# Gate logits from fp16 halves, and VectorE's five weight halves cut in two pieces each

## The chip, the cores and the metric
The kernel runs on one core of a Trainium2 chip, in one launch. The metric is the device time of that launch in microseconds. Inside the core TensorE (PE), VectorE (DVE), ScalarE (ACT) and GpSimd (POOL) run their own instruction streams, SyncE (SP) and some of the others start DMA transfers, and everything is tied together by semaphores that are written by hand.

## The reference, cut to what matters
```
x = x + attention(layernorm(x), ctx)            # 8 x 256 tokens, 512 wide, 32 heads, 8 key/value groups
h = layernorm(x)
logits = h @ gate_weight.T                      # 512 -> 8 experts, float32
scores = softmax(logits)                        # group limited: 2 of 4 groups, then top 2 of 8 experts
e_n = (silu(h @ gate_w[n].T) * (h @ up_w[n].T)) @ down_w[n].T          # n = 0..7, 352 wide
shared = (silu(h @ sh_gate_w.T) * (h @ sh_up_w.T)) @ sh_down_w.T       # 704 wide
x = x + sum_n weight_n * e_n + shared
```
The float32 products are made from fp16 halves: a value is scaled by a power of two and split as high = fp16(v), low = fp16(v - high), and three of the four half products are summed. In the kernel before, the gate logits are one of the products still made in float32 directly.

## The kernel before, in words
The 2048 tokens are 16 tiles of 128. The work runs in stages: projections and attention to about 283 us, the token stage from there to about 377 us, then the feed-forward stage (two shared experts, then 36 slots of routed rows, then the shared experts for the other half of the tokens).

**The token stage**, around which the change sits, takes the tiles in order; the numbers t below are tiles. All orders are written out by hand.
- PE, per tile t: `ln_transpose(t-2)` (L1457), `ot_transpose(t+1)` (L1440), `out_project(t)` (8 float32 instructions, L1448), `gate(t-3)` (8 float32 instructions of 8 columns with 128x128 weights, L1466). The gate waits for ACT's float32 copy of the transposed tile, `lnt_evac`. The last three gates stand between the first matmuls of the feed-forward stage.
- ACT, per tile: `lnt_out(t-2)` writes the high half of the transposed normalised tile (L1084) and a float32 copy of it, lnT (L1085); `ot_evac(t+1)` (L1079), which `out_project(t+1)` waits for; `std2(t)` (L1093), `gate_out(t-3)` (L1089), `first_part(t-2)` for t = 2 to 11, the high half of the weight half h = t-2 (L1119, after its load has landed); then `ln2_out(t)` (L1098), the normalised tile, which waits for DVE.
- DVE, per tile: `residual_norm(t)`, from the residual add (L1985) to the shift (L1994), with the low half of tile t-2 in its middle (`cut_rows`, L1971). In odd tiles 3 to 11 it then makes the low half of the weight half h = t-2 in one instruction of 1408 columns (`second_part`, L2019).
- POOL makes the low halves of the even h = 0 to 8 in two instructions of 1408 columns (scale, L838; subtract, L848), in order of h. After each h, even or odd, it starts the load of h+3 (L829, 704 KB) into the stage buffer that h has freed; for odd h it first waits for DVE's count `gu_cut_v`.
- SP, per tile: load of the attention rows of t+5, store of the two halves of tile t-2, store of the residual rows, load of the residual rows for t+2 (L563), store of the normalised rows.

The weights have been scaled by powers of two that are found in the attention stage and at the start of the token stage (`down_scales`, 10 columns, one for each expert).

## Time and profile before
| | us |
|---|---|
| median of 3 runs (753.55 to 754.98) | 754.7 |
| the profiled execution: its own time | 754.92 |
| the profiled execution: its span | 753.1 |
| PE busy | 732.2 (97%) |
| DVE busy | 561.1 (75%) |
| ACT busy | 419.0 (56%) |
| POOL busy | 272.1 (36%) |
| matmuls of the gate, L1466, x128 | 15.3 busy |

The span is what the profiler recorded from the first to the last instruction; the time is some 1.8 us longer. Busy time of an engine is an average over stages with different limits, so the stage tables and the timelines further down say more than this table. The granted clock of TensorE is 0.998 of full speed over the run.

### The profile page before, as it was taken

To read this page: it belongs to the slowest core of one execution; us is meant where nothing else is said; L and a number is where in the kernel's file an instruction comes from. 1 tells how busy PE (TensorE), PEld (TensorE's weight loads), DVE (VectorE), ACT (ScalarE), POOL (GpSimd) and SP (SyncE) were. 2 spreads that over 40 slices of the span, in tenths; PEclk is the share of its full clock that TensorE was granted. 3 is DMA by queue.
4 is the path that set the end of the run, shared out by engine and by line. 5 is a ranking of instruction groups with operands and counts; after the bars stand their busy time and mean duration, and the time that the engine had idled before them with its cause. 6 is when DMAs were issued, how large, how long until landed. Compare 5 with 4: busy or idle time off the path is not lost.

```text
span 753.1 us, 16125 instructions
## 1 busy us (share of the span) xinstructions
PE 732.2 (97%) x5325; PEld 398.9 (53%) x5326; DVE 561.1 (75%) x1191; ACT 419.0 (56%) x845; POOL 272.1 (36%) x221
## 2 busy tenths in 40 slices
PE   6998999999999999999999999999999999999998
PEld 3554533434444334656665566555555556655554
DVE  4777689999999967788589998655555555546776
ACT  3667468888888884777543454343433334223222
POOL 3264006999997311664400401212111121016540
PEclk9999999999999999999999999999999999999999
DMA  9898946755755798997578664977767779549993
GB/s 328 332 409 282 252 147 187 221 168 176 220 150 151 249 344 301 345 386 281 190 204 259 153 155 123 197 175 181 184 168 184 173 180 213 127 124 283 329 308 92
DMA packets 155100, 168.17 MB, mean 223 GB/s; under 512 B 97952, under 2 KB 111776, under 8 KB 154528
## 3 DMA queue, kind: packets, MB, share of 16 engines
q1 hardware_dynamic: 143724, 126.20, 57.6%
q0 software_dynamic: 10720, 40.12, 17.0%
q10 hardware_dynamic: 596, 1.07, 0.4%
q8 instruction: 36, 0.59, 0.4%
q14 instruction: 24, 0.20, 0.1%
HBM read 104.09 MB, written 41.42 MB: 193 GB/s over the span
## 4 chain that ended last, share of the span: by engine, by line
PE 53%; DVE 23%; DMA 8%; issue 6%; POOL 4%; ACT 3%; SPq 2%; DVEq 0%; POOLq 0%; ACTq 0%
PE psum L1521 21%; DVE sb_rows L1786 12%; PE psum L1538 11%; PE psum L1523 4%; PE psum L1448 4%; PE psum L1257 4%; POOL sb_weights L952 4%; DMA sb_weights<-k_parts 2%; DMA sb_weights<-in_wdn 2%; PE psum L1540 2%; PE psum L1233 1%; DVE sb_rows L1915 1%; PE psum L1281 1%; DMA x_dram<-sb_rows 1%; DMA sb_rows<-xb_dram 1%
## 5 line engine op out<-in xcount | busy, mean ns | idle before, releaser
L1521 PE MATMUL psum<-sb_weights,sb_rows 128*128 128x352 f16 (+1 forms) x1344 | 209.7, 313 | 0.0
L1521 PEld LDWEIGHTS psum<-sb_weights,sb_rows 128*128 128x128 f16 x1344 | 131.2, 98 | 76.1 <-issue 1.2
L1786 DVE TENSOR_REDUCE sb_rows<-psum 128x4 f32<-128x1024 f32 x128 | 150.0, 1214 | 4.6 <-PE psum L1281 4.5
L1073 ACT ACTIVATE sb_weights<-psum 128x512 f32<-128x512 f32 x256 | 139.4, 595 | 22.8 <-PE psum L1353 19.7
L1538 PE MATMUL psum<-sb_weights,sb_hT 128*128 128x512 f16 (+1 forms) x522 | 122.2, 379 | 0.0
L1147 ACT ACTIVATE psum<-psum 128x352 f32<-128x352 f32 x68 | 30.5, 448 | 124.9 <-DVE psum L2040 112.3
L933 POOL DMA_INDIRECT sb_rows<-xn_rows,sb_slot_tok x36 | 34.6, 960 | 176.7 <-DVE sb_rows L2418 134.8
L1353 PE MATMUL psum<-sb_weights 50*128 50x512 f16 x256 | 86.6, 387 | 1.7 <-ACT sb_weights L1073 0.9
L1367 PE MATMUL psum<-sb_weights 128*32 128x256 f32 x1024 | 82.6, 394 | 0.3
L1538 PEld LDWEIGHTS psum<-sb_weights,sb_hT 128*128 128x128 f16 x522 | 50.9, 98 | 54.0 <-issue 0.6
L1281 PE MATMUL psum<-sb_weights 48*128 48x256 f16 x512 | 70.7, 274 | 1.6 <-DMA sb_weights<-k_parts 0.9
L1448 PE MATMUL psum<-sb_weights 128*128 128x512 f32 x128 | 58.3, 598 | 0.5 <-ACT sb_weights L1079 0.4
L2053 DVE SCALAR_TENSOR_TENSOR sb_h<-psum,sb_h_scale_i,sb_h 128x352 f16<-128x352 f32 x68 | 39.7, 583 | 22.7 <-ACT sb_h L1152 19.5
L952 POOL DMA_INDIRECT sb_weights<-slot_y,sb_p_i x32 | 32.5, 1015 | 64.4 <-DMA slot_y<-sb_rows 41.9
L2040 DVE SCALAR_TENSOR_TENSOR psum<-psum,sb_inv_now,sb_h 128x352 f32<-128x352 f32 x36 | 21.3, 592 | 43.6 <-issue 31.0
L1353 PEld LDWEIGHTS psum<-sb_weights 50*128 50x128 f16 x256 | 23.4, 93 | 54.2 <-ACT sb_weights L1073 44.7
L1142 ACT ACTIVATE sb_h<-psum,sb_inv_now 128x352 f32<-128x352 f32 x36 | 20.0, 555 | 49.4 <-PE psum L1521 37.7
L1257 PE MATMUL psum<-sb_weights 128*128 128x512 f16 x192 | 44.9, 380 | 2.3 <-DVE sb_weights L1852 1.2
L1152 ACT ACTIVATE sb_h<-psum,sb_h_scale_i 128x352 f16<-128x352 f32 x68 | 37.7, 555 | 16.2 <-DVE sb_h_scale_i L2045 14.8
L838 POOL TENSOR_TENSOR sb_weights<-sb_weights,sb_w_scale_i 128x1408 f32<-128x1408 f32 x15 | 38.0, 2533 | 23.6 <-ACT sb_weights L1119 22.8
L848 POOL TENSOR_TENSOR sb_weights<-sb_weights 128x1408 f16<-128x1408 f32 x15 | 43.0, 2864 | 1.2
L1142 ACT ACTIVATE sb_h<-psum,sb_w_inv_i 128x352 f32<-128x352 f32 x32 | 17.8, 556 | 33.1 <-PE psum L1521 22.7
(307 smaller groups left out, 1172.8 us busy)
## 6 DMA issues: line engine op xcount, KB each, us to landing
sb_weights<-in_wgu SPq DMA_DIRECT2D x20, 704.0 KB, 7.1
sb_weights<-in_wgu POOLq DMA_DIRECT2D x20, 704.0 KB, 6.8
sb_weights<-in_wdn SPq DMA_DIRECT2D x17, 768.0 KB, 6.3
slot_y<-sb_rows SPq DMA_DIRECT2D x36, 256.0 KB, 2.4
sb_weights<-q_parts SPq DMA_DIRECT2D x96, 64.0 KB, 3.0
x_dram<-sb_rows SPq DMA_DIRECT2D x24, 256.0 KB, 4.6
q_parts<-sb_weights SPq DMA_DIRECT2D x16, 256.0 KB, 4.1
sb_rows<-in_x POOLq DMA_DIRECT2D x16, 256.0 KB, 5.8
```

Source lines behind the costliest of these rows:

```text
L848: nc.gpsimd.tensor_tensor(low, stage, high, ALU.subtract).then_inc(gu_cut, 1)
L952: nc.gpsimd.indirect_dma_start(out=to, out_offset=None, in_=slot_y, in_offset=bass.IndirectOffsetOnAxis(ap=idx[:, t:t + 1], axis=0)).then_ ...
L1073: nc.scalar.activation(probs[G % 2][:, kt, pair * 512:(pair + 1) * 512], bank[4 + f % 2], ACT.Exp, scale=exp_by[n]).then_inc(exp_done, 1)
L1257: mm = nc.tensor.matmul(bank[Q_BANKS[n][m]], wq16[:, wp, k, m * P:(m + 1) * P], xnT[n % 2][:, xp, k, :], start=(k == 0 and i == 0), stop=( ...
L1281: mm = nc.tensor.matmul(bank[banks[qt] + side][:, h * SEQ:(h + 1) * SEQ], q_st[s][lo:hi, g, h, b * SEQ + qt * P:b * SEQ + (qt + 1) * P], k ...
L1353: nc.tensor.matmul(bank[4 + side].rearrange("p (h t) -> p h t", h=HH), k_st[s][lo:hi, g, b * SEQ + kt * P:b * SEQ + (kt + 1) * P], q_st[s] ...
L1367: mm = nc.tensor.matmul(bank[6][VW * c:VW * (c + 1), 0:SEQ], v_now, probs[G % 2][:, kt, c * SEQ:(c + 1) * SEQ], start=(kt == 0), stop=(kt ...
L1448: mm = nc.tensor.matmul(bank[2 + s][:], oT[s][:, k, :], wfc_sb[:, k, :], start=(k == 0), stop=(k == KD - 1))
L1521: mm = nc.tensor.matmul(to[:, 0:F], x_T[:, at:at + P], gu(wp, k, which), start=first, stop=last)
L1538: mm = nc.tensor.matmul(bank[Y_BANKS[par]][:], hT[par][:, hp, j, :], dn(wp, j), start=first, stop=last)
L1786: nc.vector.tensor_reduce(to[:, :, j // UB, :, j % UB, qt], psum[:, banks[qt] * 512:(banks[qt] + 2) * 512] .rearrange("p (a h k) -> p a h ...
L2053: nc.vector.scalar_tensor_tensor(h16[par][:, 1, 0:F], bank[GU_BANKS[par][1]][:, 0:F], h_scale[:, par:par + 1], h16[par][:, 0, 0:F], ALU.mu ...
```

## The change
Gate: lnT and ACT's copy of it are gone. `gate(t)` multiplies both fp16 halves of the tile (high and low, which exist for the experts anyway) with one operand of 16 columns, the high and the low half of the gate weights: again 8 instructions, now fp16. The two groups of 8 sums go to two planes of `route` and are added on DVE ahead of the softmax. The gate now waits for DVE's low half (`ln16_done`) in place of ACT's copy. The scale of the gate weights is an eleventh column of the table of the down weights; its maximum is taken in the attention stage, and three small DVE instructions make the halves after tile 2 (`gate_halves`).

Pieces: the low half of an odd h was made in tile h+2; now its first 704 columns are made in tile h+2 and its last 704 in tile h+3. `gu_cut_v` counts pieces, so those who waited for h now wait for the second piece.

```
-        lnT = [row(6), row(7)]
-        xb_sb = lnT
+        xb_sb = [row(6), row(7)]
+        gw16 = wsel[...][:, 0:KD * NE].bitcast(F16).rearrange("p (k s e) -> p k s e", k=KD, s=2)
...
                 if w == 2:                                    # SP, feed-forward stage
-                    sp.wait_ge(gu_cut_v, HELD)
+                    sp.wait_ge(gu_cut_v, 2 * HELD)
...
                 else:                                         # POOL, odd h
-                    pool.wait_ge(gu_cut_v, h // 2 + 1)
+                    pool.wait_ge(gu_cut_v, h + 1)
...
-                nc.scalar.activation(ln16[s][:, 0:D], bank[4 + s][:], ACT.Copy, scale=X_SCALE)
-                nc.scalar.copy(lnT[s], bank[4 + s][:]).then_inc(lnt_evac, 1)
+                nc.scalar.activation(ln16[s][:, 0:D], bank[4 + s][:], ACT.Copy, scale=X_SCALE).then_inc(lnt_evac, 1)
...
-                nc.scalar.copy(logits[:, bass.ds(t, 1), :], bank[6 + s][:, 0:NE].unsqueeze(1)).then_inc(gate_evac, 1)
+                nc.scalar.activation(route[:, 0:2, bass.ds(t, 1), :], bank[6 + s][:, 0:2 * NE]..., ACT.Copy,
+                                     scale=dn_inv[:, NE + SH:DN_TOPS]).then_inc(gate_evac, 1)
...
             def gate(t, s):
-                pe.wait_ge(lnt_evac, t + 1)
+                pe.wait_ge(ln16_done, t + 1)
...
                 for k in range(KD):
-                    mm = nc.tensor.matmul(bank[6 + s][:, 0:NE], lnT[s][:, k * P:(k + 1) * P], gw_sb[:, k, :], ...)
+                    for part in range(2):
+                        at = part * D + k * P
+                        mm = nc.tensor.matmul(bank[6 + s][:, 0:2 * NE], ln16[s][:, at:at + P], gw16[:, k]..., ...)
...
                 if t == 3:
+                    pe.wait_ge(scale_done, 5)
                     gate(0, 0)
...
+                if G == 3:                                    # DVE, attention stage
+                    dve.wait_ge(w_fc, 48)
+                    nc.vector.tensor_reduce(dn_max[:, NE + SH:DN_TOPS], gw_sb[:]..., AX.X, ALU.max, apply_absolute_value=True)
...
+            def gate_halves():
+                g = slice(NE + SH, DN_TOPS)
+                dve.wait_ge(scale_done, 2)
+                nc.vector.tensor_scalar(dn_inv_i[:, g], dn_inv_i[:, g], float(10 << 23), None, ALU.subtract).then_inc(scale_done, 1)
+                nc.vector.tensor_scalar(gw16[:, :, 0, :], gw_sb[:], dn_scale[:, g], None, ALU.mult).then_inc(scale_done, 1)
+                dve.wait_ge(scale_done, 4)
+                nc.vector.scalar_tensor_tensor(gw16[:, :, 1, :], gw_sb[:], dn_scale[:, g], gw16[:, :, 0, :],
+                                               ALU.mult, ALU.subtract).then_inc(scale_done, 1)
...
-            def second_part(h):
+            def second_piece(h, n):
                 dve.wait_ge(gu_first, CUTS_P2 + h + 1)
                 high, low = cut_place(h)
+                here = slice(n * HALF // 2, (n + 1) * HALF // 2)
+                nc.vector.scalar_tensor_tensor(low[:, here], stage_p3[h % 3][:, here], w_scale[:, h // 2:h // 2 + 1],
+                                               high[:, here], ALU.mult, ALU.subtract).then_inc(gu_cut_v, 1)
             for t in range(2, TILES):
                 residual_norm(t, t % 2, t // 2)
-                if t % 2 == 1 and t < 2 * HELD + 2:
-                    second_part(t - 2)
+                if t == 2:
+                    gate_halves()
+                if 3 <= t < 2 * HELD + 3:
+                    h = t - 2 - (t + 1) % 2
+                    second_piece(h, (t + 1) % 2)
...
             def softmax_in():
                 dve.wait_ge(gate_evac, TILES)
+                link(nc.vector.tensor_tensor(logits, logits, score, ALU.add))
```

## Rows read from the trace of the kernel before
**Rows 1.** Stage table: stretch, busy time (instructions) per engine, clock, DMA share, GB/s.
```profile
298.00:350.00 52.00, 51.53 (x234) 31.53 (x232) 42.38 (x104) 39.01 (x69) 30.89 (x17) 1.00 1.01 368
325.00:346.00 21.00, 21.00 (x97) 13.12 (x97) 18.21 (x46) 15.70 (x29) 12.52 (x8) 1.00 1.04 385
```
**Rows 2.** Chain of waits, one tile of the token stage: start, length, what.
```profile
330.20 3.49 PE psum L1448 x8
333.69 0.79 PE psum L1466 x8
334.48 0.49 PE psum L1457 x4
334.97 0.44 PE psum L1440 x4
```
**Rows 3.** TensorE's timeline, weight loads of 32 narrow fp16 matmuls in the feed-forward stage.
```profile
426.85 0.47 PEld L1608 LDWEIGHTS psum<-sb_ln_sb,sb_rows 128*128 128x128 f16 x16
```
**Rows 4.** DVE's timeline, tiles 9 to 12.
```profile
329.38 0.68 DVE L1985 TENSOR_TENSOR sb_rows<-psum,sb_rows 128x512 f32<-128x512 f32 x1
333.73 0.69 DVE L1985 TENSOR_TENSOR sb_rows<-psum,sb_rows 128x512 f32<-128x512 f32 x1 [0.87 <-ACT sb_rows L1098]
337.25 2.64 DVE L2019 SCALAR_TENSOR_TENSOR sb_weights<-sb_weights,sb_w_scale_i 128x1408 f16<-128x1408 f32 x1
339.81 0.68 DVE L1985 TENSOR_TENSOR sb_rows<-psum,sb_rows 128x512 f32<-128x512 f32 x1
```
**Rows 5.** POOL's timeline, the even half h = 6.
```profile
332.94 2.53 POOL L838 TENSOR_TENSOR sb_weights<-sb_weights,sb_w_scale_i 128x1408 f32<-128x1408 f32 x1 [2.64 <-ACT sb_weights L1119]
335.55 2.86 POOL L848 TENSOR_TENSOR sb_weights<-sb_weights 128x1408 f16<-128x1408 f32 x1
338.70 0.58 POOL L829 DMA_DIRECT2D sb_weights<-in_wgu  x1 [0.30 <-POOL sb_weights L848]
```
**Rows 6.** The same op of DVE as in rows 4, in tiles 5 and 11, and POOL beside it.
```profile
316.68 1.69 DVE L2019 SCALAR_TENSOR_TENSOR sb_weights<-sb_weights,sb_w_scale_i 128x1408 f16<-128x1408 f32 x1 [1.11 <-ACT sb_weights L1119]
313.84 2.86 POOL L848 TENSOR_TENSOR sb_weights<-sb_weights 128x1408 f16<-128x1408 f32 x1
347.62 2.76 DVE L2019 SCALAR_TENSOR_TENSOR sb_weights<-sb_weights,sb_w_scale_i 128x1408 f16<-128x1408 f32 x1
346.04 2.86 POOL L848 TENSOR_TENSOR sb_weights<-sb_weights 128x1408 f16<-128x1408 f32 x1
```
**Rows 7.** The same kind of DVE op at 512 columns (count: min/median/max ns).
```profile
L2285 DVE SCALAR_TENSOR_TENSOR sb_weights<-sb_zero_row,sb_dn_scale_i,sb_weights x1: 741/741/741, 462.1 to 462.1; 128x512 f16<-128x512 f32 x1
```
**Rows 8.** DMA of L829: all ten (count, size, median us to landing), then those after 299 us.
```profile
sb_weights<-in_wgu POOLq DMA_DIRECT2D x10, 704.0 KB, 7.7
...
DMA to landing us min/median/max: 6.8/7.6/9.3
```
**Rows 9.** Timelines: ACT in tile 5, DVE in tile 6, and the projection of tile 8.
```profile
315.18 1.47 ACT L1119 ACTIVATE sb_weights<-sb_weights,sb_w_scale_i 128x1408 f16<-128x1408 f32 x1 [0.98 <-DMA sb_weights<-in_wgu]
318.95 0.69 DVE L1985 TENSOR_TENSOR sb_rows<-psum,sb_rows 128x512 f32<-128x512 f32 x1 [0.58 <-DMA sb_rows<-xb_dram]
324.79 3.70 PE L1448 MATMUL psum<-sb_weights 128*128 128x512 f32 x8
```
**Rows 10.** Chain of waits, from the last tile to the feed-forward stage.
```profile
364.58 0.70 DVE sb_rows L1985
369.47 0.48 ACT sb_rows L1085
371.92 3.75 PE psum L1521 x24
```
**Rows 11.** TensorE's timeline: the gate issued after the projection of tile 12.
```profile
349.17 0.95 PE L1466 MATMUL psum<-sb_gw_sb,sb_rows 128*128 128x8 f32 x8
```
**Rows 12.** Small terms: POOL's wait for the gate weights, and a 128x128 op of DVE.
```profile
116.50 0.55 POOL L872 DMA_DIRECT2D sb_rows<-in_x  x1 [0.47 <-DMA sb_gw_sb<-in_gwT]
377.74 0.29 DVE L2076 TENSOR_TENSOR sb_route<-sb_route,sb_t_tile 128x128 f32<-128x128 f32 x1
```

More of the change, by code:

```diff
@@ L81 @@
 CUT_W = 8
+DN_TOPS = NE + SH + 1
 PA, PB, PC = SH * EARLY, SLOTS, SH * (TILES - EARLY)
@@ L223, in build @@
         a_in += [dn_tail[:], bfc_sb]
-        dn_max = sb("dn_max", [P, NE + SH])
-        dn_max_all = sb("dn_max_all", [NE + SH, 1])
-        dn_exp = sb("dn_exp", [P, NE + SH], I32)
-        dn_scale_i = sb("dn_scale_i", [P, NE + SH], I32)
-        dn_inv_i = sb("dn_inv_i", [P, NE + SH], I32)
+        dn_max = sb("dn_max", [P, DN_TOPS])
+        dn_max_all = sb("dn_max_all", [DN_TOPS, 1])
+        dn_exp = sb("dn_exp", [P, DN_TOPS], I32)
+        dn_scale_i = sb("dn_scale_i", [P, DN_TOPS], I32)
+        dn_inv_i = sb("dn_inv_i", [P, DN_TOPS], I32)
         dn_scale, dn_inv = dn_scale_i[:].bitcast(F32), dn_inv_i[:].bitcast(F32)
@@ L276, in build @@
         res_in, x2_sb, xn2_sb = [row(0), row(1)], [row(2), row(3)], [row(4), row(5)]
-        lnT = [row(6), row(7)]
-        xb_sb = lnT
+        xb_sb = [row(6), row(7)]
         ln16 = [zero_row[:].bitcast(F16), ln16_sb[:].bitcast(F16)]
-        w_max_rows = row(6)[0:NE + SH, 0:P]
+        w_max_rows = row(6)[0:DN_TOPS, 0:P]
         tok_in, xT, mid, late = [row(0), row(1)], [row(2), row(3)], [row(4), row(5)], [row(6), row(7)]
@@ L305, in build @@
         wsel = sb("wsel", [P, TILES, NE])
+        gw16 = wsel[:].rearrange("p t e -> p (t e)")[:, 0:KD * NE].bitcast(F16).rearrange("p (k s e) -> p k s e", k=KD, s=2)
         sel = sb("sel", [P, TILES, NE])
@@ L1083, in lnt_out @@
                 act.wait_ge(lnt_stored[s], stored * 16 + FREE)
-                nc.scalar.activation(ln16[s][:, 0:D], bank[4 + s][:], ACT.Copy, scale=X_SCALE)
-                nc.scalar.copy(lnT[s], bank[4 + s][:]).then_inc(lnt_evac, 1)
+                nc.scalar.activation(ln16[s][:, 0:D], bank[4 + s][:], ACT.Copy, scale=X_SCALE).then_inc(lnt_evac, 1)
             def gate_out(t, s):
                 act.wait_ge(gate_ready, t + 1)
-                nc.scalar.copy(logits[:, bass.ds(t, 1), :], bank[6 + s][:, 0:NE].unsqueeze(1)).then_inc(gate_evac, 1)
+                nc.scalar.activation(route[:, 0:2, bass.ds(t, 1), :],
+                                     bank[6 + s][:, 0:2 * NE].rearrange("p (s e) -> p s e", s=2).unsqueeze(2), ACT.Copy,
+                                     scale=dn_inv[:, NE + SH:DN_TOPS]).then_inc(gate_evac, 1)
             def std2(t):
@@ L1465, in gate @@
                 for k in range(KD):
-                    mm = nc.tensor.matmul(bank[6 + s][:, 0:NE], lnT[s][:, k * P:(k + 1) * P], gw_sb[:, k, :],
-                                          start=(k == 0), stop=(k == KD - 1))
+                    for part in range(2):
+                        at = part * D + k * P
+                        mm = nc.tensor.matmul(bank[6 + s][:, 0:2 * NE], ln16[s][:, at:at + P],
+                                              gw16[:, k].rearrange("p s e -> p (s e)"),
+                                              start=(k == 0 and part == 0), stop=(k == KD - 1 and part == 1))
                 mm.then_inc(gate_ready, 1)
@@ L1481, in _ @@
                     pe.wait_ge(dn_max_done, NE + SH)
-                    nc.tensor.transpose(bank[5][0:NE + SH, 0:P], dn_max[:], ident[:]).then_inc(w_max_t, 1)
+                    nc.tensor.transpose(bank[5][0:DN_TOPS, 0:P], dn_max[:], ident[:]).then_inc(w_max_t, 1)
                 else:
                     pe.wait_ge(w_max_b, 2)
-                    nc.tensor.transpose(bank[5][:, P:P + NE + SH], w_max_rows,
-                                        ident[0:NE + SH, 0:NE + SH]).then_inc(w_max_tt, 1)
+                    nc.tensor.transpose(bank[5][:, P:P + DN_TOPS], w_max_rows,
+                                        ident[0:DN_TOPS, 0:DN_TOPS]).then_inc(w_max_tt, 1)
             for t in range(2, 4):
@@ L1652, in _ @@
             pe.wait_ge(gu_cut, CUTS - HELD)
-            pe.wait_ge(gu_cut_v, HELD)
+            pe.wait_ge(gu_cut_v, 2 * HELD)
             slot_up(0, 0)
@@ L1961, in _ @@
                     expert_scales()
+                if G == 3:
+                    dve.wait_ge(w_fc, 48)
+                    nc.vector.tensor_reduce(dn_max[:, NE + SH:DN_TOPS], gw_sb[:].rearrange("p k e -> p (k e)"), AX.X, ALU.max,
+                                            apply_absolute_value=True)
             links += link.count[0]
@@ L2014, in _ @@
             links += link.count[0]
-            def second_part(h):
+            def second_piece(h, n):
                 dve.wait_ge(gu_first, CUTS_P2 + h + 1)
                 high, low = cut_place(h)
-                nc.vector.scalar_tensor_tensor(low, stage_p3[h % 3], w_scale[:, h // 2:h // 2 + 1], high,
-                                               ALU.mult, ALU.subtract).then_inc(gu_cut_v, 1)
+                here = slice(n * HALF // 2, (n + 1) * HALF // 2)
+                nc.vector.scalar_tensor_tensor(low[:, here], stage_p3[h % 3][:, here], w_scale[:, h // 2:h // 2 + 1],
+                                               high[:, here], ALU.mult, ALU.subtract).then_inc(gu_cut_v, 1)
             for t in range(2, TILES):
                 residual_norm(t, t % 2, t // 2)
-                if t % 2 == 1 and t < 2 * HELD + 2:
-                    second_part(t - 2)
+                if t == 2:
[3 more added lines that the diff above has]
+                    second_piece(h, (t + 1) % 2)
             cut_rows(TILES - 2, 0)
```

6 lines of the change are left out of this document (3 added, 3 removed).

## The prediction
> **What bounds the kernel now.** I read the stage table first. In 298 to 350 us of the token stage TensorE idles only 0.47 of 52 us, in 325 to 346 us not at all [rows 1]; behind it, in the feed-forward stage, the page shows it at nine tenths or more in every slice. So each us that leaves TensorE in the token stage can leave the span, as long as nobody else is late. The same rows say who is near: DVE is busy 18.2 of 21 us, and the DMA share is 1.01 to 1.04.
>
> The chain of waits gives TensorE's tile: 3.49 for the projection, 0.79 for the gate, 0.49 and 0.44 for the transposes, 5.2 us together [rows 2]. The timelines of the other engines tell what their tile is. DVE takes a pair of tiles from 329.38 to 339.81, 10.43 us, in which it idles 0.87 [rows 4]. POOL and its loads are read last, since they set when a weight half can be cut at all [rows 5, 8].
>
> Two things are to be seen in these timelines. First, DVE's 1408-column op takes 1.69 us when POOL's subtract ends as it starts (313.84 + 2.86 = 316.70), but 2.64 and 2.76 when it starts inside one. In both cases it ends 1.48 after POOL's end: 338.41 to 339.89, and 348.90 to 350.38 [rows 4 to 6]. So while POOL's instruction runs, DVE's op gets only its first 0.21 us done, whatever the overlap. Second, ACT's high half of h = 3 waited for its load until 315.18 and ended at 316.65 [rows 9], and loads take 7.7 us in the median [rows 8].
>
> **Gate, on TensorE.** 8 float32 instructions of 0.79 us go, 8 fp16 ones of 16 columns come. The nearest row is a run of 128x128 fp16 weight loads with 36 columns each: 16 in 0.47 us, 0.03 each [rows 3], so 8 x 0.025 to 0.03 = 0.2 us. The gate saves 0.59 us, in 16 gates 9.4. Bounds: nothing saved if each load cost what the float32 one does (0.79/8 = 0.1), 0.6 saved at most. I take 0.59, since rows 3 are the same kind of load.
>
> The Trainium skill speaks against this. Its page "TensorE: Matmul & The Clock Gate", section on LDWEIGHTS, gives a load as columns/1.2 in ns, which is 107 ns for 128 columns, so an estimate of 0.85 us for 8 loads and no gain at all. The same page's Fast Weight Load exempts fp16 loads of 128 columns. The trace agrees with the second: 0.47 us for 16 loads [rows 3].
>
> **Gate, beside it.** ACT loses one op per tile, 0.48 us [rows 10]; it is off the path in most tiles, but on it where ACT releases the projection and at the end of the stage. The gate of tile t now waits for DVE's low half, made in tile t+2 some 2.4 us after DVE's start, and TensorE comes to it after the next projection: some 2 us of cover; if DVE falls a tile behind, TensorE stands there with the transposes and the projection behind it. The three ops of gate_halves (0.2 each with their waits, 0.65) stand on DVE after tile 2; they delay the first gate by about 0.3 and cost what that gate gains. The added 128x128 op ahead of the softmax is 0.32 [rows 12]; DVE has idle there while ACT loads its exp table, so 0, at most 0.3. The reduce in the attention stage lies on DVE where DVE is in the chain: 0.15. Its wait for w_fc would be met: POOL passed the same wait at 116.2 [rows 12], DVE would come at 116.9. The eleventh column, and 16 for 8 logits on ACT: below 0.05 per op, taken as 0.
>
> **Pieces: DVE and POOL.** From the 512- and the 1408-column op (0.74 and 1.69) a piece of 704 is 0.94 alone [rows 6, 7]. The second piece of odd h now stands at the end of the even tile h+3, and POOL, which waits for it before the load of h+3 and before its own h+1, starts later. Take the residual add of an even tile as 0:
> - the piece starts at 3.52 (337.25 - 333.73, rows 4) and ends at 4.46; DVE's next residual add can start at 4.38.
> - POOL issues the load 0.3 later and takes 0.6 for it [rows 5], so its scale starts at 5.36 (before: at 3.56, 332.94 - 329.38), its subtract 2.61 later at 7.97, and ends at 10.83 [rows 5].
> - DVE reaches the first piece of the next odd h at 4.38 + 3.52 = 7.90 at the earliest, and later than 7.97 if the odd tile waits for TensorE (tile 3.45 + 0.49 + 0.44 + 0.2 = 4.6 us) or for ACT's high half. It is a dead heat between DVE and POOL's subtract. If POOL is first, the piece ends at 10.83 + 0.73 = 11.56, and the next even tile starts at 11.5: a pair of 11.5 us against 10.43 now. If DVE is first, POOL waits 0.9 and the pair can be TensorE's 9.2.
>
> **Pieces: the loads.** The load of an odd half is issued 0.3 after POOL's subtract, lands 7.7 later, ACT's high half takes 1.47, the first piece 0.94, then a tile until the second piece's end, 4.46, then 0.9 + 5.47 until POOL's subtract has ended two pairs on. The sum is 21.2, so 10.6 us per pair; with 6.8 us for a load (the shortest of those after 299 us, rows 8) it is 10.15. So in tiles 4 to 12, where weights are cut, the pair stays between 10.15 and 11.5 by whichever of the two is met, though TensorE could do 9.2. What the gate frees there is taken by the later POOL.
>
> **The walk through the stage.** The first tiles run 0.5 earlier (copy gone from ACT ahead of the projection of tile 3, DVE's first piece instead of the whole op), so DVE starts tile 4 at 307.0, not 307.7. Tile 6 starts at 318.4 (before 318.95): the load of h = 3 is issued no earlier than now and its high half again ends at 316.65 [rows 9], inside POOL's subtract, which runs to 317.7. Then 11.4 per pair where POOL is first: 329.8, 341.2, and 351.8 for tile 12 (the last pair is shorter, as POOL issues no load in it), against 350.3 (DVE's piece of 347.62 ended then [rows 6], 1.1 after the projection of tile 12, which ended as the gate at 349.17 began [rows 11]). After tile 12 nothing is cut by POOL against DVE except the last piece. The projection of tile t+2 can start 5.36 after DVE's start of tile t (before 5.84, rows 9: 318.95 to 324.79, with the copy in it), so that of tile 14 (3.45 long) ends at 351.8 + 5.36 + 3.45 = 360.6 and that of tile 15 4.4 later, at 365.0, against 364.4: 0.6 late.
>
> At the end of the stage the chain from DVE's last tile to the second gate-up matmuls goes through ACT, not through TensorE: 364.58 to 371.92 is 7.34 us [rows 10], of which TensorE's own work is 5.2 after the change. So the gates of tiles 12 to 14 gain nothing but the copy, 0.48. The gate of tile 15 stands on TensorE's path, behind those matmuls, and gives 0.59. The sum: +0.6 - 0.48 - 0.59 + 0.15 (attention) = -0.3 us with POOL first in every pair. With DVE first in one pair, or loads of 6 us since they no longer come in twos, it is -2 to -2.5. I take -0.7, nearer the first. On the span of 753.1 that is 752.4, and with the 1.8 around it 754.2, against 754.92 of the same execution and the median of 754.7.
>
> **Rivals.**
> 1. The gain comes in part: DVE meets POOL's subtract seldom, or loads land in 6 us, and the pair in tiles 4 to 12 is near 10 us. For it: the dead heat is 0.07 us wide. Against: once DVE is late, it is late against POOL in the next pair too. The stage then gains 0.3 us per pair in four pairs and full tiles afterwards: -3.5, so 751.4.
> 2. The stage is TensorE's throughout: 16 x 0.59 less 3 x 0.59 hidden at the end, plus 0.48: -8.2, so 746.7. Against: DVE's two tiles with two pieces are 8.8 us even without POOL, and the DMA is already full at 385 GB/s [rows 1].
> 3. Slower. POOL's later start decides every pair: 4 pairs x (11.5 - 10.43) = 4.3, less 0.7 at the start, and tile 12 starts at 353; TensorE gets back 0.6 in each of the last tiles, so the last projection ends 1.9 late, +1.0 in all. Loads of 8.5 us (the longest after 299 us took 9.3, rows 8) add 1 to 2, since ACT's high half then delays the normalised tile behind it on ACT: 757. It decides as soon as pairs are above 11.2.
> 4. The change doesn't shorten the gate (weight loads at 0.1): then only the pieces act, about +2, 756.9.
>
> **How the numbers follow.** Forecast 0.42, rival 1 0.28, rival 2 0.07, rivals 3 and 4 0.19 and 0.04. What can be told from no change is 0.2%, 1.5 us. The forecast's own range is 752.9 to 755.8. Faster by more than that (below 753.2): rivals 1 and 2 and a small part of the forecast, 0.37; slower (above 756.2): rivals 3 and 4, most of them, 0.2; the same: 0.43. The range from 750.6 to 756.8 leaves out rival 2 and the far end of rival 3.
>
> **What would show it.** L1466's successor at about 0.2 us per gate, right or wrong on TensorE. In tiles 5 to 11 the first pieces at 2 to 3.5 us, ending 0.7 after POOL's subtract; if they take 0.94, the lock step is wrong. POOL's scale 5.4 us after an even residual add. Pairs of DVE's residual adds at 10.5 to 11.5 us. TensorE idle of some 1.5 us ahead of the second gate-up of the shared expert. The prediction is wrong if those pairs are below 10, if TensorE waits for `ln16_done`, or if time moves outside 298 to 377 us.

## The result, and the profile after

The changed kernel takes 758.43 us (median of 10 runs, 755.6 to 761.27) against 754.56 us for the kernel before (10 runs, 752.88 to 754.98): ratio 1.0059, interval 1.0045 to 1.0074. It is 0.6% slower, outside the range that was given. The profiled execution has a span of 756.9 us against 753.1.

The stage table comes first (columns as in [rows 1]); the last three rows are stretches inside the same stage.

```profile
298.00:350.00 52.00, 45.41 (x220) 24.30 (x219) 43.88 (x105) 30.88 (x53) 27.89 (x16) 0.97 0.97 342
350.00:385.00 35.00, 31.55 (x192) 18.21 (x191) 23.45 (x68) 22.22 (x42) 14.72 (x6) 0.95 0.58 195
336.00:338.00 2.00, 1.69 (x9) 1.36 (x10) 1.90 (x6) 1.22 (x3) 1.41 (x2) 0.79 0.98 320
338.00:342.00 4.00, 4.00 (x7) 1.58 (x6) 3.73 (x8) 3.44 (x6) 3.92 (x2) 0.68 0.92 256
372.00:376.00 4.00, 4.00 (x26) 2.27 (x25) 0.69 (x1) 2.02 (x3) 0.00 (x0) 0.66 0.57 203
```

TensorE was the bound before, 51.53 of 52 us [rows 1]. Now it idles 6.6 us of them, and for two stretches (338 to 342 and 372 to 376 us) the granted clock is about two thirds of full speed in a stage where it was 1.00. A mean of 0.66 over a stretch of a few us is a mix of the two levels, 2.4 and 1.2 GHz.

The list of TensorE's waits from 298 to 372 us (total us, times, longest) says what it idles for:

```profile
PE psum L1459 <- ACT sb_rows L1100: 5.1, 6, 1.6
PE psum L1470 <- DVE sb_ln_sb L1981: 2.5, 1, 2.5
PE psum L1470 <- DVE sb_wsel L2023: 2.0, 1, 2.0
PE psum L1470 <- DVE sb_zero_row L1981: 0.3, 1, 0.3
```

L1470 is the new gate, L1459 the transposes of the normalised tile, L2023 the last operation of gate_halves, L1981 the low half of the transposed rows (cut_rows), L1100 ScalarE's normalised tile. Each large one in its place, first the start of the stage, in the timelines of VectorE, GpSimd and TensorE:

```profile
300.56 0.23 DVE L2021 TENSOR_SCALAR sb_wsel<-sb_gw_sb,sb_dn_scale_i 128x32 f16<-128x32 f32 x1
300.60 2.58 POOL L839 TENSOR_TENSOR sb_weights<-sb_weights,sb_w_scale_i 128x1408 f32<-128x1408 f32 x1 [10.04 <-ACT sb_weights L1121]
300.83 2.40 DVE L2023 SCALAR_TENSOR_TENSOR sb_wsel<-sb_gw_sb,sb_dn_scale_i,sb_wsel 128x32 f16<-128x32 f32 x1
303.29 0.36 PE L1470 MATMUL psum<-sb_wsel,sb_zero_row 128*128 128x16 f16 x8 [2.00 <-DVE sb_wsel L2023]
```

A VectorE operation of 32 columns takes 2.40 us: it starts 0.23 us behind GpSimd's scale and ends 0.05 us behind its end (300.83 + 2.40 = 303.23, 300.60 + 2.58 = 303.18). The first gate waits 2.00 us for it.

Then the middle of the stage, TensorE's timeline at the largest of the waits for ScalarE:

```profile
334.40 0.36 PE L1470 MATMUL psum<-sb_wsel,sb_zero_row 128*128 128x16 f16 x8 [0.29 <-DVE sb_zero_row L1981]
336.31 0.66 PE L1459 MATMUL psum<-sb_ident,sb_rows 128*128 128x128 f32 x4 [1.55 <-ACT sb_rows L1100]
336.81 0.70 PE L1442 MATMUL psum<-sb_ident,sb_weights 128*128 128x128 f32 x4
337.30 5.30 PE L1450 MATMUL psum<-sb_weights 128*128 128x512 f32 x8
```

The gate itself is as forecast, about 0.2 us (the next instruction begins 0.18 to 0.20 behind it where nothing waits), but behind 1.55 us of idle the projection takes 5.30 us; with the full clock it takes 3.60 to 3.70 [rows 9]. The end of the stage has the same picture, in the timelines of TensorE and VectorE:

```profile
367.00 0.35 PE L1470 MATMUL psum<-sb_wsel,sb_zero_row 128*128 128x16 f16 x8
369.88 0.34 PE L1470 MATMUL psum<-sb_wsel,sb_ln_sb 128*128 128x16 f16 x8 [2.53 <-DVE sb_ln_sb L1981]
370.55 5.42 PE L1527 MATMUL psum<-sb_weights 128*128 128x352 f16 x24
...
375.81 0.35 PE L1470 MATMUL psum<-sb_wsel,sb_zero_row 128*128 128x16 f16 x8
```
```profile
368.95 0.68 DVE L1981 SCALAR_TENSOR_TENSOR sb_ln_sb<-psum,sb_ln_sb 128x512 f16<-128x512 f32 x1
```

The gate of tile 13 comes right behind that of tile 12, with no projection between them, and waits 2.53 us for a low half which VectorE makes only inside the norm of tile 15. The 24 gate-up matmuls behind it take 5.42 us against 3.75 [rows 10].

VectorE's pieces and GpSimd's subtracts, which answer to [rows 4 to 6]:

```profile
318.05 1.55 DVE L2040 SCALAR_TENSOR_TENSOR sb_weights<-sb_weights,sb_w_scale_i 128x704 f16<-128x704 f32 x1
319.52 0.68 DVE L1995 TENSOR_TENSOR sb_rows<-psum,sb_rows 128x512 f32<-128x512 f32 x1
322.91 0.94 DVE L2040 SCALAR_TENSOR_TENSOR sb_weights<-sb_weights,sb_w_scale_i 128x704 f16<-128x704 f32 x1
...
328.74 2.20 DVE L2040 SCALAR_TENSOR_TENSOR sb_weights<-sb_weights,sb_w_scale_i 128x704 f16<-128x704 f32 x1 [1.48 <-ACT sb_weights L1121]
331.93 0.69 DVE L1995 TENSOR_TENSOR sb_rows<-psum,sb_rows 128x512 f32<-128x512 f32 x1 [0.99 <-DMA sb_rows<-xb_dram]
...
339.83 3.51 DVE L2040 SCALAR_TENSOR_TENSOR sb_weights<-sb_weights,sb_w_scale_i 128x704 f16<-128x704 f32 x1
```
```profile
315.99 2.85 POOL L849 TENSOR_TENSOR sb_weights<-sb_weights 128x1408 f16<-128x1408 f32 x1
...
327.32 2.86 POOL L849 TENSOR_TENSOR sb_weights<-sb_weights 128x1408 f16<-128x1408 f32 x1
...
339.74 2.86 POOL L849 TENSOR_TENSOR sb_weights<-sb_weights 128x1408 f16<-128x1408 f32 x1
```

The first pieces of tiles 5 to 11 end 0.74 to 0.76 us behind GpSimd's end, whenever they start (that of tile 3 met no subtract); alone a piece takes 0.94. So half an operation took 1.55 to 3.51 us where the whole one took 1.69 to 2.76 [rows 4, 6]. The residual adds of the even tiles 4 to 12 start at 308.18, 319.52, 331.93, 343.27 and 353.83: pairs of 11.34, 12.41, 11.34 and 10.56 us.

Followed along TensorE, the loss comes in these places (start of the gate behind a tile's projection, after less before): +2.01 us behind tile 3 (303.29 against 301.28), +0.03 behind tile 6 (317.07 against 317.04), +0.87 behind tile 9 (334.40 against 333.53), +3.69 behind tile 10 (342.44 against 338.75), +2.62 behind tile 15 (367.00 against 364.38), and +4.00 at the third gate-up (380.32 against 376.32). So TensorE has made good the 2.0 us of the first gate by tile 6; 2.8 us come at tile 10, where the idle of 1.55 us and the slow projection stand together; 1.1 are made good, and the end of the stage adds 1.4. VectorE does not get back on time: its residual adds are 1.3 us late at tile 3 (303.15 against 301.84), 0.5 and 0.6 at tiles 4 and 6, 2.6 at tile 8 and 3.5 at tiles 10 and 12 (353.83 against 350.30).

### The profile page after: what moved, and what is told of

Read it like the earlier page. It is cut to its first block, busy times and chain, and to the rows that moved or that the text cites. A ratio compares the mean times of both kernels' runs of the same rounds, so it can differ in the third digit from the quotient of the medians.

```text
span 756.9 us, 16120 instructions
## 1 busy us (share of the span) xinstructions
PE 727.0 (96%) x5325; PEld 389.4 (51%) x5326; DVE 566.5 (75%) x1201; ACT 411.6 (54%) x829; POOL 271.4 (36%) x221
## 4 chain that ended last, share of the span: by engine, by line
PE 66%; DVE 18%; DMA 8%; issue 3%; ACT 2%; SPq 2%; DVEq 0%; ACTq 0%
PE psum L1527 29%; PE psum L1544 15%; DVE sb_rows L1792 9%; PE psum L1529 4%; PE psum L1259 4%; PE psum L1369 3%; DMA sb_rows<-xb_dram 3%; PE psum L1546 2%; DMA sb_weights<-in_wdn 2%; PE psum L1283 2%; PE psum L1450 2%; PE psum L1355 2%; DMA sb_weights<-k_parts 1%; PE psum L1235 1%; DVE sb_rows L1921 1%
## 5 line engine op out<-in xcount | busy, mean ns | idle before, releaser
L1450 PE MATMUL psum<-sb_weights 128*128 128x512 f32 x128 | 60.0, 613 | 0.0
L1450 PEld LDWEIGHTS psum<-sb_weights 128*128 128x128 f32 x128 | 23.7, 195 | 24.9 <-issue 24.1
```

Of the source, the lines that this page charges most:

```text
L1450: mm = nc.tensor.matmul(bank[2 + s][:], oT[s][:, k, :], wfc_sb[:, k, :], start=(k == 0), stop=(k == KD - 1))
```

## The experiments

In all of them the two transposing transfers of the feed-forward stage are plain copies of the same bytes, so their output is not the reference's. `h1_before`, the kernel before with that alone, shows what it costs.

> Base for the experiments: the kernel before, with each transposing transfer of the feed-forward stage (rows of h, slot rows) made as a plain copy of the same bytes, so what the experts multiply is not transposed. The token stage is untouched. All theories: the same 298 to 377 us as before (projection of tile 15 ends at 364 to 365 us), the whole within 1% of the kernel before, 0.99 to 1.002.

Measured: 753.73 us, ratio 1.0005 (0.9994 to 1.0016). The base is sound; ratios below are to the kernel before, 753.0 to 753.6 us on the same chip.

> The changed kernel with each transposing transfer of the feed-forward stage (rows of h, slot rows) made as a plain copy of the same bytes, so what the experts multiply is not transposed: the base for the experiments on the changed kernel. All theories: its loss against the kernel before between 298 and 380 us, as in the changed kernel itself; the whole at 757 to 760 us. Theory A: first gate 2.0 us late behind a 2.4 us op of 32 columns, pairs of DVE's residual adds of 11.3 to 12.4 us in tiles 4 to 12, 2.5 us of waiting ahead of the gate of tile 13, stretches at half clock behind idle of TensorE of 1.5 us and more.

Measured: 760.25 us over 4 executions, 1.0084 (1.0056 to 1.0112), just above the 757 to 760 said. The loss is there on this base too, if anything larger. Both waits are in its trace (1.92 us for the 32-column operation, 2.53 us ahead of gate(13)). Its profiled execution was already 2.3 us late ahead of the token stage, so its span of 759.5 us is not read against the others.

**The two halves of the change, each alone.** `h1_gate` is the change with the low half of an odd weight half in one operation:

```diff
-                if 3 <= t < 2 * HELD + 3:
-                    h = t - 2 - (t + 1) % 2
-                    second_piece(h, (t + 1) % 2)
+                if t % 2 == 1 and t < 2 * HELD + 2:
+                    second_piece(t - 2, 0)
```

`second_piece` makes all 1408 columns in it and adds 2 to `gu_cut_v`.

> Base with plain copies in place of the transposing transfers; change without the pieces: the low half of each odd h is again one op of 1408 columns in tile h+2. Theory A (three costs add up: the small op of gate_halves stands 2.0 us behind GpSimd's scale; the gate of tile 13 waits for ln16_done at the end of the stage; the pieces make long pairs): pairs in tiles 4 to 12 back to 9.8 to 10.5, both waits stay; -1 to +1 us against the base. Rival B (the pieces are the whole loss, the gate saves as I predicted): -3.5 us. Rival C (the gate part itself is the loss): +3 us or more.

Measured: 756.88 us, 1.0040 (1.0028 to 1.0053), so 3 us of loss without any piece. In its timelines both waits of the gate are there:

```profile
303.61 0.36 PE L1469 MATMUL psum<-sb_wsel,sb_zero_row 128*128 128x16 f16 x8 [2.00 <-DVE sb_wsel L2022]
```
```profile
301.14 2.40 DVE L2022 SCALAR_TENSOR_TENSOR sb_wsel<-sb_gw_sb,sb_dn_scale_i,sb_wsel 128x32 f16<-128x32 f32 x1
```

At the end gate(13) waits 2.53 us and the gate-up behind it takes 5.42. Between the gates behind tiles 4 and 12 it needs 42.73 us, the base 42.71: with these waits the shorter gate gave nothing in the middle. Theory A's size was wrong by more than 2 us, and so were its pairs (9.8 to 10.5 said; 11.99, 10.85, 10.54 and 10.59 us). The figure of rival C was met, 3.2 us over the base (756.88 - 753.73). VectorE's waits from 298 to 362 us show what made the first two of them long, a transfer that the prediction has no term for:

```profile
DVE sb_rows L1994 <- DMA sb_rows<-xb_dram: 5.3, 4, 3.2
```

These are the residual rows, 3.21 us of it at tile 5. The kernel before waited 2.3 us for them, 0.58 at tile 6 [rows 9] and 1.71 at tile 7.

`h1_pieces` is the kernel before with the two pieces alone (the same edit the other way round, and the counts that wait for it).

> Base with plain copies in place of the transposing transfers; the kernel before with the two pieces and nothing else. Theory A: first pieces end 0.73 to 0.76 after GpSimd's subtract, pairs in tiles 4 to 12 of 11.0 to 11.6, +1.5 to +2.5 us against the base. Rival B: +4 us or more. Rival C: 0 to +0.5.

Measured: 756.16 us, 1.0037 (1.0023 to 1.0050), 2.4 us over the base, as theory A said and against rivals B and C. So each half of the change costs alone, and neither is the whole loss. VectorE's pieces in it, with a residual add between:

```profile
327.43 3.65 DVE L2019 SCALAR_TENSOR_TENSOR sb_weights<-sb_weights,sb_w_scale_i 128x704 f16<-128x704 f32 x1
331.00 0.68 DVE L1984 TENSOR_TENSOR sb_rows<-psum,sb_rows 128x512 f32<-128x512 f32 x1
...
338.77 3.65 DVE L2019 SCALAR_TENSOR_TENSOR sb_weights<-sb_weights,sb_w_scale_i 128x704 f16<-128x704 f32 x1
```

```profile
327.47 2.86 POOL L847 TENSOR_TENSOR sb_weights<-sb_weights 128x1408 f16<-128x1408 f32 x1
```

The first piece began 0.04 us ahead of GpSimd's subtract by the record and was held up all the same; it ends 0.75 us behind it (331.08 against 330.33). A pair is 11.34 us there (331.00 to 342.34) against 10.43 before [rows 4].

**The two waits of the gate, taken away in turn.** `h1_halves` is the changed kernel with gate_halves ahead of VectorE's tile 2, before GpSimd starts its scale:

```diff
+            gate_halves()
             for t in range(2, TILES):
                 residual_norm(t, t % 2, t // 2)
-                if t == 2:
-                    gate_halves()
```

> Base with plain copies in place of the transposing transfers; the changed kernel with gate_halves ahead of tile 2 in place of behind it, where DVE idles for TensorE (297 us) and GpSimd has not started. Theory A: its scalar_tensor_tensor takes 0.25 us in place of 2.40, TensorE's wait of 2.0 us ahead of the first gate goes; 2 us less than the changed kernel on the same base, more if a half-clock stretch goes with it. Rivals B and C: no difference to the changed kernel on the same base.

Measured: 755.69 us, 1.0026 (1.0011 to 1.0041), 4.6 us under b8_after on another chip, 2.5 us under the changed kernel itself by the ratios (1.0059 - 1.0026). The same operation, ahead of GpSimd's work, takes a tenth of the time:

```profile
295.53 0.25 DVE L2022 SCALAR_TENSOR_TENSOR sb_wsel<-sb_gw_sb,sb_dn_scale_i,sb_wsel 128x32 f16<-128x32 f32 x1
```

It is 2.40 us in the four traces that have it beside GpSimd's scale and 0.25 in the others, which have it ahead. The first gate starts at 300.57 with no wait. What stays is the wait at the end, but this time at the full clock; instead the clock falls in the middle of the stage, behind a shorter idle. TensorE's timeline:

```profile
345.39 0.66 PE L1458 MATMUL psum<-sb_ident,sb_rows 128*128 128x128 f32 x4 [1.55 <-ACT sb_rows L1099]
345.88 0.81 PE L1441 MATMUL psum<-sb_ident,sb_weights 128*128 128x128 f32 x4
346.49 5.13 PE L1449 MATMUL psum<-sb_weights 128*128 128x512 f32 x8
...
368.02 0.34 PE L1469 MATMUL psum<-sb_wsel,sb_ln_sb 128*128 128x16 f16 x8 [2.53 <-DVE sb_ln_sb L1980]
...
368.70 3.74 PE L1526 MATMUL psum<-sb_weights 128*128 128x352 f16 x24
```

`h2_tail` is the changed kernel with gate(13) behind the first gate-up, on TensorE (and its copy on ScalarE in the same way):

```diff
-            gate(TILES - 3, 1)
             ln_transpose(TILES - 2, 0)
             early_up(0, 0, 0, 0)
+            gate(TILES - 3, 1)
             gate(TILES - 2, 0)
```

> The changed kernel with one edit: TensorE's gate(13), and ScalarE's gate_out(13) with it, stand behind the first gate-up of the feed-forward stage instead of ahead of it, where the changed kernel has them right behind gate(12). In the feed-forward stage the two transposing transfers are plain copies of the same bytes, as in the other kernels of this group. Theory A (the idle 2.5 us of TensorE between gate(12) and gate(13), and the half clock of the first gate-up behind it, 5.4 us instead of 3.7, cost most of the last 1.4 us of the loss): no wait of more than 1 us ahead of a gate at the end of the stage, the first gate-up begins within 0.5 us behind the last projection's gate, and the time falls by 1.2 to 3 us against the changed kernel, ratio to the kernel before 1.003 to 1.007. Rival B (the first gate-up waits for its own input or weights anyway): the wait moves to the gate-up, the time moves by less than 0.5 us.

Measured: 756.60 us, 1.0046 (1.0025 to 1.0068). The ratio is inside theory A's range, but the gain against the changed kernel is 1.0 us by the ratios (1.2 to 3 said) and the intervals overlap, so the trace has to say it:

```profile
367.20 0.35 PE L1469 MATMUL psum<-sb_wsel,sb_zero_row 128*128 128x16 f16 x8
...
369.33 3.75 PE L1526 MATMUL psum<-sb_weights 128*128 128x352 f16 x24 [0.97 <-DMA sb_weights<-xnT_dram]
372.92 0.35 PE L1469 MATMUL psum<-sb_wsel,sb_ln_sb 128*128 128x16 f16 x8
```

From the gate of tile 12 to the end of the first gate-up it is 5.7 us (372.92 - 367.20) against 8.8 before the edit (375.81 - 367.00), to the start of the third gate-up 11.1 (378.27 - 367.20) against 13.3 (380.32 - 367.00). The expectation that the first gate-up begins within 0.5 us behind the last projection's gate was wrong: it begins 2.1 us behind that gate's start. 0.97 us of the wait has moved to the gate-up's own input, as rival B says, and in the changed kernel it was hidden behind the longer one.

`h2_halves_tail` has both edits and keeps the pieces; `h2_all` has both and the whole operation.

> The changed kernel with both edits: gate_halves ahead of VectorE's tile 2, and gate(13) behind the first gate-up; the five operations stay in two pieces. Plain copies for the two transposing transfers. Theory A (of the loss some 4 us are these two waits with the half clock behind them; what the pieces cost, 2.4 us when added alone to the kernel before, is met by what the shorter gate saves): ratio 0.998 to 1.002, that is 751.8 to 754.8 us. Theory C (the pieces keep VectorE late until the end of the stage and TensorE follows it): the time stays where gate_halves alone has brought it, 755 to 756.5 us.

> Only the shorter gate: the change without the two pieces, gate_halves ahead of tile 2, gate(13) behind the first gate-up. Plain copies for the two transposing transfers. Theory A (the gate's 0.59 us a tile is worth something once its own preparation and the last gate's wait are out of TensorE's way): 750.5 to 752.8 us, ratio 0.9965 to 0.9995, and faster than the same with pieces by 1 to 2 us. Theory D (TensorE follows VectorE's pairs of tiles, so the shorter gate is worth nothing in the middle): within 0.5 us of the kernel before, with TensorE's waits for the normalised tile's output on ScalarE in place of the gate's time.

Measured: 753.57 us, 1.0000 (0.9985 to 1.0014), and 751.32 us, 0.9981 (0.9962 to 1.0001). The two waits, with the lower clock behind them, are worth 4.4 us together (1.0059 to 1.0000), as theory A has it and against theory C, which is as much as the whole loss; the pieces cost another 1.4 us by the ratios, 2.2 by the medians. The four versions agree as a square: without the waits it is 4.4 us less with the pieces and also without them (1.0040 to 0.9981), and without the pieces 1.4 us less both times, though each step of 1.4 is smaller than the two intervals it lies between. With b8_after in place of the changed kernel (1.0084) the two would be 6.3 and 3.3 us. What is left for the shorter gate is 1.4 us, not 9, and its interval just reaches 1; its trace has 2.7 us, as below. TensorE's waits in `h2_all`, 298 to 372 us:

```profile
PE psum L1458 <- ACT sb_rows L1099: 5.7, 6, 1.3
PE psum L1526 <- DMA sb_weights<-xnT_dram: 1.0, 1, 1.0
PE psum L1526 <- ACT sb_route L1088: 0.3, 1, 0.3
```

The 0.6 us that each gate gives back come again as waits for the normalised tile, for ScalarE follows VectorE. VectorE in turn:

```profile
325.53 3.21 DVE L2038 SCALAR_TENSOR_TENSOR sb_weights<-sb_weights,sb_w_scale_i 128x1408 f16<-128x1408 f32 x1 [0.47 <-ACT sb_weights L1120]
330.39 0.68 DVE L1980 SCALAR_TENSOR_TENSOR sb_zero_row<-psum,sb_zero_row 128x512 f16<-128x512 f32 x1
...
335.87 3.39 DVE L2038 SCALAR_TENSOR_TENSOR sb_weights<-sb_weights,sb_w_scale_i 128x1408 f16<-128x1408 f32 x1 [0.27 <-ACT sb_weights L1120]
340.91 0.68 DVE L1980 SCALAR_TENSOR_TENSOR sb_zero_row<-psum,sb_zero_row 128x512 f16<-128x512 f32 x1
```

Its operation of 1.69 us [rows 6] takes 3.2 to 3.4 here, since it meets GpSimd's subtract in every pair (it ends some 1.48 us behind it each time); the pair is 10.52 us (340.91 - 330.39) against 10.43 before [rows 4]. Between the gates behind tiles 4 and 12 it is 41.87 us (306.18 to 348.05) against 42.71, at the third gate-up 2.7 us are gained (373.88 against 376.62 in h1_before). So theory D for the middle of the stage, where 0.8 of them are, and theory A for its ends and for the time.

**What sets the pace then.** `h2_best` adds one step to `h2_all`: ScalarE makes the high half ahead of the tile's standard deviation, so that GpSimd starts earlier.

```diff
+                if t - 2 < 2 * HELD:
+                    first_part(t - 2)
                 std2(t)
                 if t >= 3:
                     gate_out(t - 3, (t - 3) % 2)
-                if t - 2 < 2 * HELD:
-                    first_part(t - 2)
```

> As the kernel with only the shorter gate, and one step more: ScalarE issues first_part(t-2) ahead of the standard deviation of tile t instead of behind it, so that GpSimd's scale and subtract of an odd tile begin earlier. Plain copies for the two transposing transfers. Theory D (the pair of tiles on VectorE sets the pace, and in it the wait of VectorE's operation of the low half for GpSimd's subtract): GpSimd begins 1 to 1.4 us earlier, VectorE's whole operation takes 2.2 us or less instead of 2.9 to 3.4 in the odd tiles, the pairs fall below 10.4 us, and the time by 2 to 5 us against the kernel before: 748 to 751.5 us. Rival E (the lock only moves to another pair of operations): the pairs stay at 10.4 to 10.5, the time within 1 us of the kernel with only the shorter gate.

Measured: 751.69 us, 0.9974 (0.9952 to 0.9995), not to be told from `h2_all`, though VectorE's operation of the low half takes 1.68 us in every odd tile of its trace. The pairs did not fall below 10.4 us as theory D said (10.67, 11.37, 10.11 and 11.10). What VectorE waits for in its place, from 298 to 362 us:

```profile
DVE sb_rows L1994 <- DMA sb_rows<-xb_dram: 9.2, 6, 2.9
DVE sb_rows L1994 <- PE psum L1449: 2.2, 2, 1.6
```

9.2 us for the residual rows, for which `h2_all` has no wait in this stretch; the kernel before has 2.3 us and `h1_gate` 5.3. Rival E had the right size by another mechanism: not another lock, but a transfer. `h3_best_load` issues that load earlier, and `h3_all_load` does so without the first_part step:

```diff
+                sp.wait_ge(x2_done, t + 1)
+                load_res_rows(t // 2 + 1, s)
                 store_lnT(t - 2, s)
                 store_x2(t, s)
-                load_res_rows(t // 2 + 1, s)
                 store_xn2(t, s)
```

> The kernel of the last experiment (only the shorter gate, gate_halves ahead of tile 2, gate(13) behind the first gate-up, first_part(t-2) ahead of the standard deviation), and SyncE issues the load of a tile's residual rows (res_in) as soon as VectorE has added the tile before it, ahead of the stores of the transposed rows, some 2.5 us sooner. Plain copies for the two transposing transfers. Theory F (with the lock gone, VectorE's next wait is for these rows, 1.3 to 2.9 us at four tiles): these waits fall below 1 us, the pairs of tiles below 10 us, and the time by 1.5 to 4 us against the kernel with only the first_part step, that is 747.5 to 750 us. Rival G (the DMA queues are full through this stage, 361 to 370 GB/s and share 1.00 in 298 to 350 us in every one of these kernels, so that an earlier load only takes the bandwidth of another): the wait moves to another transfer, and the time stays within 0.7 us.

> Only the shorter gate (without pieces, gate_halves early, gate(13) late), with the same earlier load of the residual rows and without the first_part step. Plain copies for the two transposing transfers. Theory D (VectorE's operation of 3.2 to 3.5 us behind GpSimd's subtract sets the pairs here, there is no wait for the rows in its trace): the load changes nothing, within 0.7 us of the kernel without it (751.3 us). Rival: more than 1 us faster, then the loads were in the way all the same.

Measured: 750.38 us, 0.9966 (0.9949 to 0.9984), and 751.19 us, 0.9975 (0.9960 to 0.9990). In the first the wait for the rows is gone from the list, and another transfer stands there, the store out of the buffer that the add writes:

```profile
DVE sb_rows L1995 <- DMA x_dram<-sb_rows: 5.2, 4, 2.5
DVE sb_rows L1995 <- PE psum L1450: 4.8, 6, 1.6
```

Its stage table may say why each repair gives so little:

```profile
298.00:350.00 52.00, 49.38 (x247) 26.92 (x245) 41.52 (x110) 34.19 (x60) 30.92 (x17) 1.00 1.00 374
```

The DMA engines are busy throughout, at 374 GB/s against 368 before [rows 1]. That they are the next bound is argued from this share; no version moved fewer bytes. It is rival G for the mechanism and, by the ratios, for the size: 0.6 us less than `h2_best` (0.9974 to 0.9966; by the medians, from two chips, 1.3), and of the pairs only the last is below 10 us. `h3_all_load` is within 0.7 us of `h2_all`, as theory D said. The gains of the single steps (0.7 us for first_part, from `h3_all_load`, 0.6 for the load, from `h2_best`) are smaller than their intervals; only their sum, from the kernel before to this one, is measured: -2.6 us by the ratio 0.9966.

The same two steps on the kernel before, each alone:

> The kernel before with the earlier load of the residual rows alone. Plain copies for the two transposing transfers. TensorE was busy for 51.3 of the 52 us of 298 to 350 us and set the pace, so both theories expect no change, within 0.7 us of the kernel before; a gain would say that part of what the other kernels of this call win is the load alone.

> The kernel before with first_part(t-2) ahead of the standard deviation alone. Plain copies for the two transposing transfers. Theory D with TensorE as the bound (51.3 of 52 us busy): VectorE's operation of the low half is 1.7 us in all odd tiles instead of up to 2.7, and the time doesn't move, within 0.7 us of the kernel before. Rival: the few waits that the stage has (the kernel before is 1 us over TensorE's own work) go, up to 1 us faster.

Measured: 752.85 us, 0.9992 (0.9976 to 1.0007), as expected, and 754.28 us, 1.0015 (1.0000 to 1.0030), 1.1 us more where 0.7 at most was expected. The twelve executions of the second fall in two groups by their mean granted clock: 754.94 to 756.48 us at 0.995 and 0.997 (six), 751.25 to 753.62 at 0.998 and 1.00 (six); what brings the one or the other was not looked for. Neither edit shows a gain while TensorE is the bound (52.00 of 52 us busy from 298 to 350 in both traces). Of the 2.6 us, 1.4 are there without either edit (`h2_all`), and the rest was seen only beside the shorter gate.

## Why the prediction was wrong

**The steps that failed.** Three, all about what stands around the gate, none about the gate:

1. "The three ops of gate_halves (0.2 each with their waits, 0.65) ... delay the first gate by about 0.3 and cost what that gate gains." They were priced as if alone. The third reads two operands in SBUF and fell beside GpSimd's scale; beside GpSimd's subtract the prediction had itself found VectorE's larger operation to stand still. It took 2.40 us, and the first gate waited 2.00. Moved ahead of GpSimd's work it takes 0.25, and the time falls by 2.5 us (h1_halves).
2. "TensorE comes to it after the next projection: some 2 us of cover." True in the tiles, where the wait for cut_rows was 0.29 us once; false at the end, where the gates of tiles 12 and 13 stand back to back. There it was 2.53 us. The text even named a wait for `ln16_done` as what would make it wrong, and did not walk the last three gates. The idle of some 1.5 us that it looked for ahead of the second gate-up is not there.
3. An idle was counted at its length; the granted clock is in no term of the sum. Behind 1.55 and 2.53 us of idle the next matmuls ran at the lower clock and took 5.30 and 5.42 us in place of 3.7, 1.6 to 1.7 more each time.

The rows show of step 1 that the small operation lasted until GpSimd's instruction was over. The Trainium skill, page "SBUF — State Buffer", section "SBUF: two separate sides", says why: the port pair that VectorE and GpSimd share is a lock held for a whole instruction, which a VectorE operation with two SBUF inputs needs too. The 2.40 us agree. The section also says that whoever starts first gets it; the piece of h1_pieces that began 0.04 us ahead does not bear this out, if the records are that exact. Of step 3 the rows show stretches at 0.66 to 0.79 of the clock behind an idle TensorE. The Trainium skill, page "TensorE: Matmul & The Clock Gate", section "HAM oscillation — how this bites in real kernels", describes this: waits between bursts of matmuls bring the lower clock back, and the next burst starts in it. The waits of its example are longer than these. The traces agree that it happens, but not behind every wait: 2.53 us of idle in h1_halves had 3.74 us behind it.

**The steps that held.** The gate: 0.79 to 0.18 - 0.20 us, as taken. The lock step of the pieces: end 0.74 to 0.76 behind GpSimd's (0.73 said); pairs of 11.4, 11.4, 11.4 and 10.6 said, 11.34, 12.41, 11.34 and 10.56 measured. GpSimd was first in every pair, once by 0.09 us only (339.74 against 339.83), and h1_pieces shows that a piece beginning at the same instant loses too.

**Where the sum went off.** The first even tiles came at 308.18 and 319.52 instead of 307.0 and 318.4, late by step 1: tile 4 stands 11.08 us behind tile 2 (297.10), and 9.65 in h1_halves, which is what 307.0 had. In the pair of 12.41 us VectorE waited 1.48 us for ScalarE's high half, as "the loads" had feared, and 0.99 for the residual rows, for which the prediction has no term; that is 1.0 us more. So the projection of tile 15, said to end at +0.6, ended at +2.6. What the end of the stage adds, said at -1.1, was +1.4: 2.5 more, from step 2 and the clock behind it, less what was hidden. The forecast's sum for GpSimd first in every pair, -0.3, with these 2.0 and 2.5 in it is +4.2; measured are +4.00 at the third gate-up and +3.8 on the span. Two readings of rows were off without effect on the sum: the 128x128 operation takes 0.29 us, not 0.32, and GpSimd's transfer stands at 116.50, not 116.2 [rows 12].

**The rivals.** Rival 3 (slower, pairs above 11.2) has the sign, and its tile 12 is right: 350.3 + 4.3 - 0.7 is 353.9 (it writes 353), measured 353.83. But it ends at +1.0, for it has neither step 2 nor step 3, and the pieces that it rests on cost 2.4 to 2.8 us alone (h1_pieces) and 1.4 to 2.2 beside the mended gate, less than the 4.4 of the two waits. The forecast had the same pairs of 11.4 us, so the pairs do not tell it from rival 3, whatever its "above 11.2" says. Rival 1 fails on the pairs and rival 4 on the gate's 0.2 us. Rival 2 (TensorE's stage throughout) is refuted for every version: the shorter gate with its two long waits gone and without the pieces gains 1.4 us of 9.4, since VectorE with GpSimd keeps its pair of 10.5 us, and behind it stand the transfers. The loss of the gate alone (3 us, h1_gate) had no rival: the prediction gave the gate a value of nothing or more in every case.

**What stays open.** How much of the loss is the lower clock by itself was not separated: the versions without the waits are also those without the fall. The mean granted clock of each execution says that it may be much of it. Of the ten executions of the changed kernel nine have 0.988 to 0.993 and took 756.79 to 761.27 us; the tenth has 1.00 and took 755.60, about 1 us over the kernel before. Of the 99 executions of the kernel before that stand beside the runs of h1, h2 and h3 none is under 0.995; beside h1 the nine at 1.00 have a median of 752.31 us and the thirteen at 0.995 one of 753.58. One execution is little to rest on, and the mean is over the whole run, in which the attention stage has lower clocks too (0.97 from 103 to 160 us, before and after). Which of TensorE's idles brings the fall is open too. The six traces with the change (the changed kernel, b8_after, h1_gate, h1_halves, h2_tail, h2_halves_tail) have 17 waits of TensorE of 1.53 to 2.53 us from 298 us to the first gate-up. Six had the lower clock behind them: 3 of 9 of 1.53 to 1.63 us, 1 of 4 of 1.92 to 2.00, 2 of 4 of 2.53. So moving an idle can move the fall, as h1_halves did. Why h1_halves gives 2.5 us, when TensorE was on time again at tile 6 of the changed kernel, is open with it. The best version was measured only with plain copies for the two transposing transfers.

## What to carry to other kernels

When an edit puts an operation on the engine next to the bound, walk its first and its last use: cover that is there in the steady part of a loop is missing where the loop is entered and left, and here two such waits cost as much as the whole loss. Even an operation of 32 columns that VectorE makes from two operands in SBUF cost the rest of GpSimd's instruction it fell into, so it belongs ahead of GpSimd's work. And splitting such an operation in pieces doesn't shorten the wait: the piece ended 0.75 us behind GpSimd, the whole one 1.48, and the second piece, 0.94 us, is extra. Where TensorE's idles can bring the lower clock, look at the clock column behind each of them in the new trace before pricing the change by the idle alone.

## What the runs showed of the hardware

- VectorE's operation of 128x32, two operands in SBUF, took 2.40 us when it started 0.23 us behind a GpSimd instruction of 2.58 us, and 0.25 us with none beside it (h1_halves); the one before it in the program, of the same size but with one tensor operand, took 0.23 us, of which 0.19 lay beside that instruction.
- The first piece, of 704 columns, took 1.43 to 3.65 us when it began well inside GpSimd's subtract or beside its start, always ending some 0.75 us behind it, and 0.94 alone. One that began 0.21 us before the subtract's end took 0.96 (h1_halves).
- Eight fp16 matmuls of 16 columns, each with its 128x128 weight load, took 0.18 to 0.20 us in the chain of waits, eight float32 ones of 8 columns 0.79.
- TensorE's granted clock fell behind some idles of 1.55 to 2.53 us (6 of 17 waits of 1.53 to 2.53 in six traces), in a stage where it is 1.00 otherwise, and the next matmuls took 4.86 to 5.42 us in place of 3.7; an equal idle of 2.53 us left it alone in two other traces (h1_halves, b8_after).
- The DMA share from 298 to 350 us was 0.96 to 1.01 in all versions, at 341 to 374 GB/s, whichever engine was late.
